# A query's own scores and weights: from five 512-column fp32r products to 32-column fp32 products and a round trip through device memory

## The chip, the cores and the metric

The kernel runs on one core of one Trainium2 chip. The metric is the device time of one execution in microseconds (us), lower is better; the times given are the median of three executions and, for the trace, the one execution that was profiled.

## What is computed

The reference applies two conditional residual layers to `x` (8 batches of 512 rows by 512 features). The change lies in the first, an attention layer with 16 heads of 32 features:

```python
query = seq2 + b_self
key   = concatenate([seq1 + b_prev, seq2 + b_self], 1)      # seq1 = x, seq2 = the side input
value = concatenate([seq1, seq2], 1)
q, k, v = query @ Wq + bq, key @ Wk + bk, value @ Wv + bv   # split in 16 heads of 32
score_prev = einsum('bhqd,bhkd->bhqk', q, k[:, :, :512]) * SCALE      # masked behind seq_len1
score_self = (q * k[:, :, 512:]).sum(-1, keepdims=True) * SCALE       # one score per query: its own key
weights = softmax(concatenate([score_prev, score_self], -1))
attn = einsum(weights[..., :-1], v[:, :, :512]) + weights[..., -1:] * v[:, :, 512:]
x = x + (attn @ Wo + bo)
```

So each query has 512 scores against the previous sequence and one score against itself (the **own score**). The second layer is an MLP with a shared and an expert part, `gelu(x @ W1 + b1) @ [W2 | We[index]]`, added to `x`. The change does not touch it.

## The kernel before

**Stages.** Everything stands transposed: features on the 128 partitions, the 512 rows of a batch along the free axis. The first stage computes the attention of all 8 batches and writes it to device memory; the second does the output projection, the residual and the MLP. Products that need precision are made of three fp32r products (high by high, high by low, low by high parts).

**Runs.** The attention stage is a sequence of 32 *runs*, one for each batch b and group g of four heads (g is 0 to 3; C = 4 groups in a batch, G = 4b + g counts them). The functions `batch` of each engine (TensorE from line 1220, ScalarE 664, VectorE 925, GpSimd 528, SyncE's queue 374) are loops over g with 16 *steps* i inside. The first and the last batch are unrolled, the six between them are a hardware loop. Nothing is scheduled at run time: each engine works down its own list, and semaphores hold it where its input isn't there. In what follows "run g" is the run of group g in a middle batch and "step i" one of its 16 steps.

**What TensorE does in a step.** One score tile of the present group (`score_tile`, line 1167: keys 128t to 128t+127 of head j against 512 queries, i = 4t + j); at most two `max_tile` products of the *next* group (1129; VectorE's `maximum`, 826, takes the row maxima off them, and product n waits until maximum n-2 is made), 16 in steps 0 to 9; from step 4 a third of one of four projections for the group after the next (`project`, 1084, four products a step); at steps 1, 5, 9 and 13 a `value_burst` (1176: four fp32 products of probabilities by values, each in 32 columns of the array), at step 5 also `denominators` (1189: four of the same form). In run 0 of a batch steps 1 to 4 hold also `values` (1114: 12 products each). The score tile of step i waits until ScalarE has made the probabilities of step i-2, since there are two banks of scores.

**The softmax bound and the own score.** The exponent is taken relative to a bound per query, the larger of its maximum over the keys and its own score. For the next group this is prepared in the present run:
- VectorE's `qk` (813) makes q times own key, `qk_f`; ScalarE's `qk_high` (578, step 1 of the next run) and VectorE's `qk_low` (822, step 5) split it into fp32r parts.
- At step 10 TensorE's `own_scores` (1142) sums it over each head's 32 features: two products of 512 columns with the 4-column matrix `sum_heads`, into 4 rows of `ps_max[1]`. `turn_max` (1150) turns the column maxima `m_col` into 4 rows of `ps_max[0]` by four fp32 products of 128 columns with the identity.
- ScalarE's `own_row` (589) copies the 4 rows, VectorE's `max_row` (835) takes the larger, ScalarE's `m_high` (595) and VectorE's `m_low` (842) make the negative high and low part in `m_neg`, and ScalarE's queue issues two DMAs (`maxima`, 603, at step 12) that put them into two rows of `q_st`, from where the score products subtract them. The first score tile of the next run waits for them (`m_landed`, 1171).
- At step 13 TensorE's `own_less_max` (1157) makes own score minus bound on all 128 rows at once: two products with the 128x128 block matrix `sum_spread` and one of `spread` by `m_neg`. ScalarE's `own_weight` (611, step 15) takes the exponential of it into `den`, waiting first for VectorE's `normalize` (884) of step 14, which frees that half of `den`.
- In the next run GpSimd's `own_value` (493, step 3) multiplies the own values by it, VectorE's `numerator` (847, step 3) and `denominator` (856, step 7) add it in. The first burst of that run waits for `numerator`, which frees `ps_num`.

**SyncE's queue** holds in each run the DMAs that stack the parts of the group after the next (`stack`, 311: three of 128 KB for each of four heads, and one row of the mask for groups 0 and 1), which wait for `q_low` at step 11; in run 1 also the loads of the next batch (`load`, 301), of which two are placed before head 0's and two before head 2's stacks; and last `store` (325) of the group before. ScalarE has in runs 1 and 2 also the `in_high` casts of the next batch, VectorE their transposes and GpSimd their low parts.

Of the kernel before, what the change touches and what calls it, by code (L numbers as in the profile page):

```python
# [19 lines left out]
def cond_resid_program(nc, x, seq2, prev_len, expert, Wq, bq, Wk, bk, Wv, bv, Wo, bo, b_prev, b_self,  # L20
# [16 lines left out]
    KE = DH + HG  # L37
# [3 lines left out]
    attn_dram = nc.dram_tensor("attn_scratch", (B, C, P, S), F32, kind="Internal").ap()  # L41
    mask_dram = nc.dram_tensor("mask_scratch", (B, S), F32, kind="Internal").ap()
# [15 lines left out]
    with keep:  # L58
# [37 lines left out]
        spread_f = before.enter_context(nc.sbuf_tensor("spread_f", [KE, P], F32))  # L96
# [16 lines left out]
        qk_hi = sb1("qk_hi", [P, S], F32R)  # L113
        qk_lo = sb1("qk_lo", [P, S], F32R)
        m_row = sb1("m_row", [HG, S])
        m_neg = sb1("m_neg", [KE, S], F32R)
        m_col = sb1("m_col", [P, C, HG])
        sum_heads = sb1("sum_heads", [P, HG], F32R)
        sum_spread = sb1("sum_spread", [P, P], F32R)
        spread = sb1("spread", [KE, P], F32R)  # L120
# [65 lines left out]
        qk_f_made, qk_hi_made, qk_lo_made = sem("qk_f_made"), sem("qk_hi_made"), sem("qk_lo_made")  # L186
# [5 lines left out]
        m_row_made, m_hi_made, m_lo_made = sem("m_row_made"), sem("m_hi_made"), sem("m_lo_made")  # L192
        m_landed = [sem(f"m_landed{r}") for r in range(2)]
        ow_mm, ow_made = sem("ow_mm"), sem("ow_made")
# [99 lines left out]
        def _(sp):  # L294
# [29 lines left out]

            def store(b, c):
# [42 lines left out]
            for j in range(HG):  # L368
                stack(0, 1, j)
            for dst, src in ((bv_col[:, :], bv), (bo_col[:, :], bo), (bias_1[:, :], b1), (bias_2[:, 0:CS], b2)):  # L370
# [104 lines left out]
        def _(pool):  # L475
            pool.memset(ident_f[:, :], 0.0).then_inc(consts_made, 1)
            pool.memset(spread_f[:, :], 0.0).then_inc(consts_made, 1)
            pool.iota(pos_i[:, :], pattern=[[1, S]], base=0, channel_multiplier=0).then_inc(consts_made, 1)
            pool.wait_ge(consts_made, 2)
            pool.affine_select(out=ident_f[:, :], in_=ident_f[:, :], compare_op=ALU.not_equal, fill=1.0, base=0,  # L480
                               pattern=[[-1, P]], channel_multiplier=1).then_inc(consts_made, 1)
            for n in range(2):

                pool.wait_ge(consts_made, 4 + n)
                pool.affine_select(out=spread_f[:, :].rearrange("k (j d) -> k j d", d=DH),
                                   in_=spread_f[:, :].rearrange("k (j d) -> k j d", d=DH),
                                   compare_op=ALU.not_equal, fill=1.0, base=-QUAD * n,
# [859 lines left out]
```

## Time and profile before

| | |
|---|---|
| median of 3 executions | 1920.85 us (1918.96 to 1922.35) |
| the profiled execution | 1924.15 us, span in the trace 1922.3 us |
| TensorE busy (PE) | 1838.3 us, 96% of the span |
| VectorE (DVE) busy | 965.4 us, 50% |
| ScalarE (ACT) busy | 752.9 us, 39% |
| GpSimd (POOL) busy | 636.2 us, 33% |
| mean granted TensorE clock | 0.977 of full |

The attention stage lasts from the start to about 1100 us, the MLP stage from there to the end. A run of groups 1 or 3 takes 28.8 us, a run of group 0 some 38.6 us, since it holds `values`. "PEld" are weight loads, which overlap the products; "ACTq" and "SPq" are the engines' queues, which issue DMAs in order with their other instructions. The printed duration of a product is longer than its place in the stream: two fp32r products of 512 columns that follow each other are printed with 0.39 us each and start 0.23 us apart, so the starts are to be read.

### The profile page before, as it was taken

How to read it: one execution, taken by the hardware profiler on the slowest of the kernel's cores; microseconds unless marked ns; L12 is line 12 of the kernel's file. 1: busy time of each engine (PE TensorE's matmuls, PEld its weight loads, DVE VectorE, ACT ScalarE, POOL GpSimd, SP SyncE). 2: the span in 40 equal slices, each digit the busy share in tenths (PEclk: the TensorE clock that was granted, in tenths of full speed). 3: DMA queues.
4: the chain of work that ended last, by engine and by line, in shares of the span. 5: the costliest groups of instructions: out<-in, count | busy, mean ns of one | idle time of the engine just before them, and what ended most of it. 6: DMA issues, size and time to landing. Idle time of an engine off the chain costs nothing.

```text
span 1922.3 us, 27293 instructions
## 1 busy us (share of the span) xinstructions
PE 1838.3 (96%) x8288; PEld 1300.6 (68%) x8288; DVE 965.4 (50%) x1373; ACT 752.9 (39%) x1290; POOL 636.2 (33%) x492
## 2 busy tenths in 40 slices
PE   6999999999999999999998799999999999999997
PEld 5656656556566565565564378888888888888886
DVE  4576576775775757757757552313232323232311
ACT  3354454444544544445434432323333332323222
POOL 3276484674764846747646400000000000000000
PEclk8999999999999999999999599999999999999999
DMA  6152342431623324316223431212131212122111
GB/s 142 35 116 57 70 83 71 78 82 39 121 59 73 78 67 82 77 40 120 64 53 88 126 94 39 50 38 50 33 55 33 50 37 38 47 33 51 27 22 22
DMA packets 337244, 122.17 MB, mean 64 GB/s; under 512 B 285642, under 2 KB 304074, under 8 KB 337170
## 3 DMA queue, kind: packets, MB, share of 16 engines
q1 hardware_dynamic: 336658, 120.83, 29.3%
q10 hardware_dynamic: 512, 0.53, 0.1%
q8 instruction: 26, 0.43, 0.1%
q14 instruction: 48, 0.39, 0.1%
HBM read 53.63 MB, written 16.79 MB: 37 GB/s over the span
## 4 chain that ended last, share of the span: by engine, by line
PE 85%; DVE 5%; issue 3%; POOL 3%; ACT 2%; SPq 2%; DMA 1%; ACTq 1%; DVEq 0%; POOLq 0%
PE ps_proj L1109 17%; PE ps_av L1061 6%; PE ps_av L1063 6%; PE ps_av L1062 6%; PE ps_av L1186 6%; PE ps_max L1139 6%; PE ps_score L1173 5%; PE ps_proj L1061 3%; PE ps_max L1063 3%; PE ps_score L1063 3%; PE ps_score L1062 3%; PE ps_max L1062 3%; PE ps_max L1061 3%; PE ps_score L1061 3%; PE ps_proj L1062 3%
## 5 line engine op out<-in xcount | busy, mean ns | idle before, releaser
L626 ACT ACTIVATE p_f<-ps_score 128x512 f32<-128x512 f32 x512 | 305.7, 599 | 499.3 <-PE ps_score L1173 415.7
L832 DVE TENSOR_REDUCE m_col<-ps_max 128x1 f32<-128x512 f32 x512 | 331.6, 684 | 237.8 <-PE ps_max L1139 237.4
L510 POOL TENSOR_TENSOR p_sum<-p_sum,p_f 128x512 f32<-128x512 f32 x256 | 344.1, 1357 | 113.8 <-ACT p_f L626 112.8
L994 DVE TENSOR_TENSOR h_lo<-h_f,h_hi 128x512 fp32r<-128x512 f32 x128 | 88.3, 690 | 480.0 <-ACT h_hi L723 479.9
L507 POOL TENSOR_TENSOR p_sum<-p_f 128x512 f32<-128x512 f32 x128 | 163.1, 1296 | 267.7 <-PE ps_av L1195 260.0
L1173 PE MATMUL ps_score<-stacks 99*128 99x512 f32 x512 | 216.8, 426 | 10.3 <-ACT p_f L626 9.6
L1139 PE MATMUL ps_max<-stacks 97*128 97x512 f32 x512 | 190.7, 428 | 31.6 <-DVE m_col L832 28.5
L1109 PE MATMUL ps_proj<-in_hi,w_hi 128*128 128x512 f32 x512 | 208.0, 406 | 10.9 <-POOL in_lo L515 7.6
L1109 PE MATMUL ps_proj<-in_lo,w_hi 128*128 128x512 f32 x512 | 206.4, 403 | 0.0
L1109 PE MATMUL ps_proj<-in_hi,w_lo 128*128 128x512 f32 x512 | 206.2, 403 | 0.0
L1061 PE MATMUL ps_av<-y_hi,w_hi 128*128 128x512 f32 x512 | 199.4, 390 | 1.5 <-DVE y_lo L990 1.5
L1063 PE MATMUL ps_av<-y_hi,w_lo 128*128 128x512 f32 x512 | 199.2, 389 | 0.0
L1062 PE MATMUL ps_av<-y_lo,w_hi 128*128 128x512 f32 x512 | 199.2, 389 | 0.0
L721 ACT ACTIVATE h_f<-ps_av,bias 128x512 f32<-128x512 f32 x128 | 88.2, 689 | 243.1 <-PE ps_av L1063 216.5
L723 ACT ACTIVATE h_hi<-ps_av,bias 128x512 fp32r<-128x512 f32 x128 | 88.2, 689 | 208.2 <-PE ps_max L1063 208.2
L1139 PEld LDWEIGHTS ps_max<-stacks 97*128 97x128 f32 x512 | 97.5, 190 | 104.6 <-DVE m_col L832 85.6
L1186 PE MATMUL ps_av<-p_f,v_st 128*32 128x512 f32 x1024 | 144.3, 627 | 5.0 <-ACT p_f L626 4.9
L1173 PEld LDWEIGHTS ps_score<-stacks 99*128 99x128 f32 x512 | 97.5, 191 | 74.9 <-ACT p_f L626 39.7
L1109 PEld LDWEIGHTS ps_proj<-in_hi,w_hi 128*128 128x128 f32 x512 | 97.9, 191 | 55.1 <-issue 32.8
L1109 PEld LDWEIGHTS ps_proj<-in_hi,w_lo 128*128 128x128 f32 x512 | 97.6, 191 | 45.4 <-issue 25.2
L1109 PEld LDWEIGHTS ps_proj<-in_lo,w_hi 128*128 128x128 f32 x512 | 97.9, 191 | 41.5 <-issue 25.1
L882 DVE RECIPROCAL den<-den 128x128 f32<-128x128 f32 x128 | 112.2, 918 | 0.7
(129 smaller groups left out, 2863.3 us busy)
## 6 DMA issues: line engine op xcount, KB each, us to landing
stacks<-parts SPq DMA_DIRECT2D x384, 128.0 KB
raw<-in_x_dram SPq DMA_DIRECT2D x128, 64.0 KB, 2.1
raw<-in_fside_BxSxS_dram SPq DMA_DIRECT2D x128, 64.0 KB, 2.2
attn_scratch<-num SPq DMA_DIRECT2D x32, 256.0 KB, 2.3
x_raw<-in_x_dram SPq DMA_DIRECT2D x128, 64.0 KB, 2.1
a_raw<-attn_scratch SPq DMA_DIRECT2D x32, 256.0 KB, 3.2
we_raw<-in_L_cond_We_dram SPq DMA_DIRECT2D x32, 256.0 KB, 2.8
out_dram<-z_t SPq DMA_DIRECT2D x128, 64.0 KB, 1.9
```

The costliest lines, as they stand in the source:

```text
L507: pool.tensor_tensor(p_sum[:, j], p_f[:, j], now, ALU.add).then_inc(sum_made, 1)
L510: pool.tensor_tensor(p_sum[:, j], p_sum[:, j], now, ALU.add).then_inc(sum_made, 1)
L626: act.activation(p_f[:, i % FLIGHT], ps_score[i % 2][:, :], ACT.Exp, scale=SCALE).then_inc(p_made, 1)
L832: dve.tensor_reduce(m_col[:, n % C, n // C:n // C + 1], ps_max[n % 2][:, :], AX.X, ALU.max).then_inc(max_made, 1)
L882: dve.reciprocal(den[:, r, at], den[:, r, at]).then_inc(rden_made, 1)
L1061: pe.matmul(ps, left[0], right[0], start=first, stop=False)
L1062: pe.matmul(ps, left[0], right[1], start=False, stop=False)
L1063: return pe.matmul(ps, left[1], right[0], start=False, stop=last)
L1109: mm = pe.matmul(ps, left, right, start=(m == 0), stop=(m == 3 * C - 1))
L1139: pe.matmul(ps_max[n % 2][:, :], q_st[0:KM, r, j, P * t:P * (t + 1)], k_st[0:KM, r, j, :], start=True, stop=True).then_inc(max_mm, 1)
L1173: pe.matmul(ps_score[i % 2][:, :], k_st[0:KS, r, j, P * t:P * (t + 1)], q_st[0:KS, r, j, :], start=True, stop=True).then_inc(score_mm, 1)
L1186: pe.matmul(ps_num[at, :], v_st[:, t, P * g + DH * j:P * g + DH * (j + 1)], p_f[:, i % FLIGHT], start=(t == 0), stop=(t == C - 1)).then_in ...
```

## The change

It replaces the 4-row tiles of own scores and maxima by one 128x128 tile: row 32t + j, column q is head j, query 128t + q.
- `own_scores` becomes four fp32 products of 128 columns, one for each quarter t, each into 32 rows of `ps_max[1]`; `turn_max` likewise into `ps_max[0]`. `sum_heads` and `m_col` are 32 columns wide, zero beyond the fourth. `qk_hi`, `qk_lo`, `qk_high` and `qk_low` go.
- `own_less_max` goes from TensorE; VectorE subtracts on the 128x128 tile. ScalarE takes the exponential in place and stores the tile to device memory, and SyncE's queue spreads each head's row to 32 rows of `den` with four DMAs.
- `maxima` issues eight DMAs (quarter t, high or low) where it issued two.
- TensorE's value bursts and the denominators stand one step later and behind the projections, VectorE's `numerator` and `denominator` one step later. At step 10 the burst stands right before `own_scores` and `turn_max`.

```diff
+    own_dram = nc.dram_tensor("own_scratch", (2, C, DH, P), F32, kind="Internal").ap()
...
+            def own_weights(b, c):
+                G, r = C * b + c, c % 2
+                sp.wait_ge(ow_stored, DMA * (G + 1))
+                wait(sp, attn_made, G - 1)
+                for j in range(HG):
+                    sp.dma_start(den[DH * j:DH * (j + 1), r].rearrange("d (t q) -> d t q", q=P),
+                                 own_dram[r, :, j].partition_broadcast(DH)).then_inc(ow_landed[r], DMA)
...
@@ SyncE, batch: behind the stacks, before store
+                    if not (last and g == C - 1):
+                        own_weights(*after(b, g, 1))
...
@@ GpSimd
             def own_value(b, c):
-                pool.wait_ge(ow_made, G + 1)
+                pool.wait_ge(ow_landed[c % 2], HG * DMA * (2 * b + c // 2 + 1))
...
@@ ScalarE
-            def qk_high(b, c):
...
-                act.copy(m_row[:, :], ps_max[1][0:HG, :]).then_inc(own_made, 1)
+                wait(act, ow_stored, DMA * G)
+                act.copy(own_s[:, :], ps_max[1][:, 0:P]).then_inc(own_made, 1)
...
-                act.mul(m_neg[0:HG, :], m_row[:, :], -1.0).then_inc(m_hi_made, 1)
+                act.mul(m_neg[:, 0], m_s[:, :], -1.0).then_inc(m_hi_made, 1)
...
                 for n in range(2):
-                    act.dma_start(f(q_st[KM + n:KM + n + 1, r]),
-                                  f(m_neg[QUAD * n:QUAD * n + HG])).then_inc(m_landed[r], DMA)
+                    for t in range(C):
+                        act.dma_start(f(q_st[KM + n:KM + n + 1, r, :, P * t:P * (t + 1)]),
+                                      f(m_neg[DH * t:DH * t + HG, n])).then_inc(m_landed[r], DMA)
 
             def own_weight(b, c):
-                act.wait_ge(ow_mm, G + 1)
-                wait(act, attn_made, G - 1)
-                act.activation(den[:, c % 2], ps_max[1][:, :], ACT.Exp, scale=SCALE).then_inc(ow_made, 1)
+                act.wait_ge(own_less_made, G + 1)
+                act.activation(own_s[:, :], own_s[:, :], ACT.Exp, scale=SCALE).then_inc(ow_made, 1)
+                pb, pc = after(b, c, -2)
+                wait(act, ow_landed[c % 2], HG * DMA * (2 * pb + pc // 2 + 1))
+                act.wait_ge(ow_made, G + 1)
+                act.dma_start(own_dram[c % 2].rearrange("t k q -> (t k) q"), own_s[:, :]).then_inc(ow_stored, DMA)
...
@@ VectorE
-            def qk_low(b, c):
...
-                dve.tensor_tensor(m_row[:, :], ps_max[0][0:HG, :], m_row[:, :], ALU.max).then_inc(m_row_made, 1)
+                dve.tensor_tensor(m_s[:, :], ps_max[0][:, 0:P], own_s[:, :], ALU.max).then_inc(m_s_made, 1)
...
+            def own_less_max(b, c):
+                dve.wait_ge(m_s_made, C * b + c + 1)
+                dve.tensor_tensor(own_s[:, :], own_s[:, :], m_s[:, :], ALU.subtract).then_inc(own_less_made, 1)
...
-                        if i == 3 and started:
+                        if i == 4 and started:
                             numerator(*after(b, g, -1))
-                        if i == 7 and started:
+                        if i == 8 and started:
                             denominator(*after(b, g, -1))
...
@@ TensorE
-                pe.matmul(ps_max[1][0:HG, :], sum_heads[:, :], qk_hi[:, :], start=True, stop=False)
-                pe.matmul(ps_max[1][0:HG, :], sum_heads[:, :], qk_lo[:, :], start=False, stop=True).then_inc(own_mm, 1)
+                for t in range(C):
+                    mm = pe.matmul(ps_max[1][DH * t:DH * (t + 1), 0:P], sum_heads[:, :], qk_f[:, P * t:P * (t + 1)],
+                                   start=True, stop=True)
+                mm.then_inc(own_mm, 1)
...
-                    mm = pe.matmul(ps_max[0][0:HG, P * t:P * (t + 1)], m_col[:, t, :], f(ident[:, :]), start=True, stop=True)
+                    mm = pe.matmul(ps_max[0][DH * t:DH * (t + 1), 0:P], m_col[:, t, :], f(ident[:, :]), start=True, stop=True)
...
-            def own_less_max(b, c):
...
-                        if i == 1 and not (first and g == 0):
-                            value_burst(*after(b, g, -1), C - 1)
-                        if i > 1 and i % HG == 1:
-                            value_burst(b, g, i // HG - 1)
-                        if i == HG + 1 and not (first and g == 0):
-                            denominators(*after(b, g, -1))
                         if g == 0 and not first and 1 <= i < 1 + C:
                             values(b, i - 1)
                         if more and i >= 4:
                             project(*nxt2, order[(i - 4) // 3], (i - 4) % 3)
+                        if i == 2 and not (first and g == 0):
+                            value_burst(*after(b, g, -1), C - 1)
+                        if i > 2 and i % HG == 2:
+                            value_burst(b, g, i // HG - 1)
+                        if i == HG + 2 and not (first and g == 0):
+                            denominators(*after(b, g, -1))
                         if bound and i == 10:
                             own_scores(*nxt)
                             turn_max(*nxt)
-                        if bound and i == 13:
-                            own_less_max(*nxt)
```

## Rows read from the trace of the kernel before

**Rows 1.** The page's busy times, and the window of a run 3.

```profile
PE 1838.3 (96%) x8288; PEld 1300.6 (68%) x8288; DVE 965.4 (50%) x1373; ACT 752.9 (39%) x1290; POOL 636.2 (33%) x492
...
419.60:448.40 28.80, 28.08 (x135) 16.56 (x134) 21.19 (x29) 13.60 (x25) 16.97 (x14) 1.00 0.28 65
```

**Rows 2.** TensorE's timeline, run 3, steps 10 to 14: start, duration, instruction.

```profile
438.69 0.40 PE L1147 MATMUL ps_max<-qk_hi,sum_heads 128*4 128x512 f32 x1
...
439.25 1.04 PE L1154 MATMUL ps_max<-ident,m_col 128*4 128x128 f32 x8
440.22 0.50 PE L1173 MATMUL ps_score<-stacks 99*128 99x512 f32 x1
440.56 0.40 PE L1109 MATMUL ps_proj<-in_lo,w_hi 128*128 128x512 f32 x1
...
444.99 0.39 PE L1163 MATMUL ps_max<-qk_hi,sum_spread 128*128 128x512 f32 x1
...
445.98 0.50 PE L1173 MATMUL ps_score<-stacks 99*128 99x512 f32 x1
```

**Rows 3.** TensorE's timeline, run 3, step 5: a burst, the denominators, then projections.

```profile
427.43 1.06 PE L1186 MATMUL ps_av<-p_f,v_st 128*32 128x512 f32 x8
428.31 1.04 PE L1195 MATMUL ps_av<-p_sum,ones 128*32 128x512 f32 x8
429.29 0.50 PE L1109 MATMUL ps_proj<-in_lo,w_hi 128*128 128x512 f32 x1
429.62 0.39 PE L1109 MATMUL ps_proj<-in_hi,w_lo 128*128 128x512 f32 x1
```

**Rows 4.** TensorE's timeline, run 2: the score tiles of steps 12 and 15.

```profile
412.65 0.40 PE L1173 MATMUL ps_score<-stacks 99*128 99x512 f32 x1
...
418.42 0.39 PE L1173 MATMUL ps_score<-stacks 99*128 99x512 f32 x1
```

**Rows 5.** ScalarE's timeline, run 2: probabilities 12, the two DMAs, probabilities 13.

```profile
413.08 0.60 ACT L626 ACTIVATE p_f<-ps_score 128x512 f32<-128x512 f32 x1
414.63 1.22 ACTq L608 DMA_DIRECT2D stacks<-m_neg  x2
416.05 0.60 ACT L626 ACTIVATE p_f<-ps_score 128x512 f32<-128x512 f32 x1 [2.37 <-POOL p_sum L510]
```

**Rows 6.** DMA issues by line: duration on the queue in ns, minimum, median, maximum.

```profile
L608 ACTq DMA_DIRECT2D stacks<-m_neg x64: 580/587/1182, 69.4 to 1052.2; - x64
...
L323 SPq DMA_DIRECT2D stacks<-parts x384: 552/598/2155, 37.8 to 1028.0; - x192
...
L308 SPq DMA_DIRECT2D raw<-in_x_dram x128: 316/348/1792, 2.7 to 881.4; - x128
```

**Rows 7.** SyncE's queue, run 2: the last three of the stacks' DMAs.

```profile
420.97 1.87 SPq L323 DMA_DIRECT2D stacks<-parts  x3
```

**Rows 8.** The page's DMA issues: KB each, median us to landing.

```profile
raw<-in_x_dram SPq DMA_DIRECT2D x128, 64.0 KB, 2.1
...
attn_scratch<-num SPq DMA_DIRECT2D x32, 256.0 KB, 2.3
```

**Rows 9.** GpSimd's and VectorE's timelines, start of run 3, and all maxima by line.

```profile
421.21 1.28 POOL L498 TENSOR_TENSOR v<-v,den 128x512 f32<-128x512 f32 x1
...
425.67 0.68 DVE L853 TENSOR_TENSOR num<-ps_av,v 128x512 f32<-128x512 f32 x1
...
L832 DVE TENSOR_REDUCE m_col<-ps_max 128x1 f32<-128x512 f32 x512 | 331.6, 684 | 237.8 <-PE ps_max L1139 237.4
```

**Rows 10.** A product's idle time at the start of run 2, and windows.

```profile
389.91 0.49 PE L1139 MATMUL ps_max<-stacks 97*128 97x512 f32 x1 [0.79 <-DVE m_col L832]
...
396.00:398.00 2.00, 2.00 (x9) 0.90 (x8) 1.75 (x4) 0.83 (x2) 1.21 (x1) 0.50 0.07 26
398.00:400.00 2.00, 2.00 (x17) 0.49 (x16) 1.37 (x3) 0.27 (x1) 0.00 (x0) 0.68 0.00 0
...
779.50:781.00 1.50, 1.50 (x5) 1.11 (x5) 1.08 (x2) 0.00 (x0) 1.07 (x1) 0.50 0.01 3
```

More of the change, by code:

```diff
@@ L36, in cond_resid_program @@
     KS = KM + 2
-    KE = DH + HG
     QUAD = 32
@@ L191, in cond_resid_program @@
         turn_mm = sem("turn_mm")
-        m_row_made, m_hi_made, m_lo_made = sem("m_row_made"), sem("m_hi_made"), sem("m_lo_made")
+        m_s_made, m_hi_made, m_lo_made = sem("m_s_made"), sem("m_hi_made"), sem("m_lo_made")
         m_landed = [sem(f"m_landed{r}") for r in range(2)]
-        ow_mm, ow_made = sem("ow_mm"), sem("ow_made")
+        own_less_made, ow_made = sem("own_less_made"), sem("ow_made")
+        ow_stored = sem("ow_stored")
+        ow_landed = [sem(f"ow_landed{r}") for r in range(2)]
         score_mm = sem("score_mm")
@@ L476, in _ @@
             pool.memset(ident_f[:, :], 0.0).then_inc(consts_made, 1)
[L477 removed]
             pool.iota(pos_i[:, :], pattern=[[1, S]], base=0, channel_multiplier=0).then_inc(consts_made, 1)
[L479 removed]
+            pool.wait_ge(consts_made, 1)
             pool.affine_select(out=ident_f[:, :], in_=ident_f[:, :], compare_op=ALU.not_equal, fill=1.0, base=0,
                                pattern=[[-1, P]], channel_multiplier=1).then_inc(consts_made, 1)
[L482 to L487, printed above, removed]
[L488 removed]
+            pool.wait_ge(consts_made, 3)
             pool.memset(f(stacks[KM - 1:KS, 1]), 1.0).then_inc(ones_made[1], 1)
@@ L576, in v2_out @@
                 act.copy(v2[:, c], ps_proj[0][:, :]).then_inc(v2_made, 1)
-            def qk_high(b, c):
-                G = C * b + c
-                act.wait_ge(qk_f_made, G + 1)
-                wait(act, ow_mm, G)
-                act.copy(qk_hi[:, :], qk_f[:, :]).then_inc(qk_hi_made, 1)
             def v_out(b, t):
@@ L649, in _ @@
             weights_high(2)
-            qk_high(0, 0)
             v2_out(0, 0)
@@ L676, in batch @@
                             v2_out(*nxt)
-                        if i == 1 and maximum:
-                            qk_high(*nxt)
                         if g == 0 and not first and 2 <= i < 2 + C:
@@ L912, in _ @@
             weights_low(2, 2)
-            qk_low(0, 0)
             for t in range(3 * C):
@@ L921, in _ @@
             qk(0, 1)
-            max_row(0, 0)
+            own_max(0, 0)
             m_low(0, 0)
+            own_less_max(0, 0)
             def batch(b, first, last):
@@ L934, in batch @@
                                 maximum(*nxt, n)
-                        if i == 5 and bound:
-                            qk_low(*nxt)
-                        if i == 3 and started:
+                        if i == 4 and started:
                             numerator(*after(b, g, -1))
-                        if i == 7 and started:
+                        if i == 8 and started:
                             denominator(*after(b, g, -1))
@@ L951, in batch @@
                             m_low(*nxt)
+                            own_less_max(*nxt)
                         if i in (10, 13) and started:
@@ L1170, in score_tile @@
                 if i == 0:
-                    pe.wait_ge(m_landed[r], 2 * DMA * (2 * b + g // 2 + 1))
+                    pe.wait_ge(m_landed[r], 2 * C * DMA * (2 * b + g // 2 + 1))
                 wait(pe, p_made, T - 1)
@@ L1214, in _ @@
             values(0, 1)
-            own_less_max(0, 0)
             values(0, 2)
```

64 lines of the change are left out of this document (23 added, 41 removed).

## The prediction

> **What bounds the kernel now.** First the page's busy times and one run's window: TensorE is busy in 96% of the span, and in a run 3 of 28.8 us in 28.1, while VectorE, ScalarE and GpSimd stand at 75% of that window or less [rows 1]. So TensorE's stream sets the time, and what leaves it is gained, as long as nobody else is then late. Second, that stream itself, read by its starts. A product of 512 columns takes 0.23 us. I count a run 3 by this: 16 score tiles, 16 maxima and 48 projections are 80 x 0.23 = 18.5 us; four bursts of 1.2 us, 4.8; the denominators 0.9; what the change touches 2.7 (below). That is 26.9 of 28.8; the other 1.9 us are short stalls, nearly all in steps 0 to 5, where TensorE has few projections and waits for VectorE's maxima at 0.65 us each. Third, ScalarE in steps 12 to 15, the only place where the change puts more work on an engine's queue than it takes away.
>
> **Removed from TensorE.** From the first own product to the score tile behind the turned maxima are 440.22 - 438.69 = 1.53 us, and the product behind that tile starts 0.34 us after it and not 0.23: 1.64 us [rows 2]. `own_less_max`: 445.98 - 444.99 = 0.99, and 0.11 again: 1.10 us [rows 2]. Together 2.74 us a run.
>
> **Added there.** Eight fp32 products of 128 columns, each four in four different 32-column blocks. No row shows these. The denominators have this form with 512 columns: the burst's four take 0.88 us before them, in which the four ran side by side, since the turned maxima, four products of 128 columns in one and the same block, take 0.97 us for a quarter of the columns [rows 2, 3]. A quarter of 0.88 is 0.22 us for each set of four: 0.44. The upper bound is that they don't run side by side: 2 x 0.97 = 1.94. I take 0.44, as rows 3 have the same form. They stand behind a burst and cost no change of form of their own. The bursts are only moved: five places of 1.2 us or less, as before. **Net on TensorE: 2.74 - 0.44 = 2.3 us a run, 32 runs: -74 us.**
>
> **ScalarE's queue.** This is where I expect the gain to go. `maxima` issues eight DMAs for two. The two take 1.22 us back to back, and the probabilities of step 13 come only behind them [rows 5]. What would eight smaller ones take? An issue of 8 KB takes 0.587 us there, one of 128 KB on SyncE's queue 0.598; the cheapest loads from device memory take 0.316 [rows 6]. So it is the price of an instruction and not of its bytes, and both 0.59 rows go from SBUF to SBUF, as the new ones do. I take 0.61 each: 4.9 us; the lower bound is 0.32 each, 2.5 us.
> The path: score tile 12, then 0.43 us to its probabilities (412.65 to 413.08), 0.6 us for them, 4.9 us of issues, 0.2 to the next activation (415.85 to 416.05), 0.6 for probabilities 13 and 0.05 for the signal: 6.8 us until score tile 15 may start [rows 4, 5]. (The low part is ready by then: on 128 columns VectorE's small steps cost less than on 512.) TensorE has three steps of 5 x 0.23 and one burst between them, 4.65 us; before, it needed 5.77 [rows 4], with `own_less_max` among it. So it stands idle for 2.15 us, in 31 runs: **+66 us**. In run 1 two `in_high` casts (0.6 us each) stand on the same stretch; half of that has no cover: +0.7 x 8 = +6.
>
> By the Trainium skill (DMA: Bandwidth & Descriptors, Rules for kernel authors) small transfers should be coalesced, since under 64 KB one pays mostly overhead. The trace agrees in the issue times above, 0.587 us for 8 KB. If an issue went by its bytes instead, the eight would cost what the two cost, 1.2 us, and the term of 66 us would be nothing.
>
> **Step 15.** Exponential and store (0.3 and 0.4 us, the latter like other issues to device memory) stand before probabilities 15, which score tile 1 of the next run needs. ScalarE's wait for `normalize` goes to SyncE's queue. From probabilities 13 on: 14, exponential, store, 15 are 2.1 us, against 1.15 + 0.7 us on TensorE: +0.35 x 31 = **+11**.
>
> **Steps 0 to 5.** The burst leaves step 1 for step 2 and then stands under maxima already queued; the `qk_low` and `qk_high` passes go. I reckon VectorE's chain as 4.8 us from tile 0 to tile 4 for 5.3 now, and some of it comes back at maximum 7: -0.7 in 16 runs (1 and 3; run 2 has transposes there): **-11**. In run 0 `v_out` needs the burst that now stands behind `values(1)`: `values(2)` waits burst end + copy (0.6) less three products (0.7) and signals, 0.5 x 7: **+4**.
>
> **The own weight's way through memory.** Counted from score tile 15: probabilities 13 end with it, the store is issued 1.3 us later, lands 2.3 us on [rows 8] (3.6). SyncE's queue: its last stack waits for score tile 15 and has three issues, 1.9 us [rows 7]; with the mask rows it is full till about 3.2. Then four loads at 0.35 to 0.54, landing 2.1 after the last issue [rows 6, 8]: 7.1. GpSimd's product 1.3, so `numerator` can start at 8.5 and ends at 9.2 [rows 9], which is 8 us behind score tile 0. Now GpSimd's product starts 1.7 us behind that tile (421.21; the tile is at 419.56) and the numerator at 6.1 [rows 9]. VectorE stands before maximum 8 so long, and TensorE's product 10 (step 6, 8.5 us behind tile 0) needs it: about +0.5 us in run 1, 0.7 in run 3. In run 2 SyncE has 8 loads more before the last stacks, but GpSimd is behind there already: +1.0. Run 0 hides it behind `values`. 2.2 x 8 = **+18**. Bounds: 0 and 2.5 us in each of 24 runs, +60.
> At step 6 the denominators are 1.6 us later; GpSimd's first sum of `p` then is ready about 0.5 us before probabilities 8 want it: 0.
>
> **The clock.** In run 2 TensorE waited 0.79 us and twice more [rows 10], and then the granted clock stood at 0.50 for 2 us and at 0.68 over the next 2: 0.5 x 2 + 0.32 x 2 = 1.6 us lost [rows 10]. 0.50 is the lower of its two levels, 1.2 for 2.4 GHz. I find three such falls in the middle of the stage, near 140, 396 and 780 us, the last in these rows too. The new kernel idles 2.15 us in one piece at step 14: some more falls, six or so: **+10**.
>
> **Sum:** -74 + 66 + 6 + 11 - 11 + 4 + 18 + 10 = +30. Against the profiled execution 1924 + 30 = 1954; the median lies 3.3 lower: **1951 us**, 1.6% slower. What a measurement can tell from no change is about 0.2%, 4 us.
>
> **Rivals.**
> - *Issues are cheap* or there is slack that I don't see: at 0.32 us each ScalarE needs 4.4 us for the 4.65, so the 66, the 6 and most of the 11 go: 1951 - 80 = 1871; at 0.47 some 1910. For it: loads at 0.316. Against: the same line now shows a minimum of 0.580 in 64 issues. It ends faster; it decides below 0.49 us an issue (0.12 x 8 = 1 us less a run), where the sum is zero. With smaller errors of the other terms in the same direction, 0.34, centre 1895.
> - *The clock follows the idle stretch* in most runs, not in a few: 25 falls of 1.6 us, +40, less my 10: 1981. For it: three falls, each behind idle time of this size. Against: in run 3, with idle pieces of 0.3 us, none. 0.15.
> - *The 32-column blocks queue up*: +1.5 x 32 = 48: 1999. Against: rows 3. 0.04.
> - *It cancels*: 0.08.
> - My forecast, 0.39, own range 1930 to 1970.
>
> Slower is 0.39 + 0.15 + 0.04 = 0.58, faster 0.34, same 0.08. Two in ten left out, one on each side, gives 1878 to 1990: the lower end takes in an issue price near 0.35 us [rows 6], the upper one the clock.
>
> **What would show it.** Line 608's successor: 256 issues at 0.58 us; score tile 15 idle about 2 us on ScalarE's probabilities in nearly every run; the page's four-block products x8 in about 0.22 us for a set; TensorE's share falling from 96% to about 93%; VectorE's numerator waiting for GpSimd, and that for the loads into `den`. Wrong if the issues take half, if TensorE doesn't wait at step 15, or if the stage ends before 1060 us.

## Result, and the profile after

The changed kernel takes 2066.7 us (median of four, 2061.4 to 2068.0) against 1921.0 for the kernel before on the same chip: ratio 1.0754 (95% interval 1.0733 to 1.0775), 146 us slower. I had forecast 30 us slower with an upper end of 1990: the sign is right, the size is far off. The profiled execution's span is 2064.7 us against 1922.3.

First the page of the changed kernel: the engines' busy time, and the chain that ended last.

```profile
PE 1835.2 (89%) x8384; PEld 1320.9 (64%) x8384; DVE 981.5 (48%) x1367; ACT 712.8 (35%) x1258; POOL 618.1 (30%) x489
...
PE 74%; ACTq 8%; DVE 6%; issue 5%; POOL 3%; ACT 2%; SPq 1%; DMA 1%; POOLq 0%; DVEq 0%
```

TensorE's busy time is 3 us less than before [rows 1], its share 89% for 96%. So its idle time rose by (2064.7 - 1835.2) - (1922.3 - 1838.3) = 145.5 us, which is all of the 142 us by which the span grew. But the busy time should have fallen by the 74 us of work removed. That it did not is seen in the groups of products that the change leaves alone (busy us, mean ns of one, idle time before):

```profile
L1157 PE MATMUL ps_score<-stacks 99*128 99x512 f32 x512 | 246.4, 482 | 164.7 <-ACT p_f L625 163.4 <-DMA stacks<-m_neg 1.2
L1101 PE MATMUL ps_proj<-in_hi,w_hi 128*128 128x512 f32 x512 | 215.3, 420 | 23.6 <-POOL in_lo L517 20.3
L1131 PE MATMUL ps_max<-stacks 97*128 97x512 f32 x512 | 208.8, 471 | 13.1 <-DVE m_col L821 12.7
```

The same three groups in the kernel before:

```profile
L1173 PE MATMUL ps_score<-stacks 99*128 99x512 f32 x512 | 216.8, 426 | 10.3 <-ACT p_f L626 9.6 <-DMA stacks<-m_neg 0.6
L1109 PE MATMUL ps_proj<-in_hi,w_hi 128*128 128x512 f32 x512 | 208.0, 406 | 10.9 <-POOL in_lo L515 7.6 <-DVE w_lo L796 3.2
L1139 PE MATMUL ps_max<-stacks 97*128 97x512 f32 x512 | 190.7, 428 | 31.6 <-DVE m_col L832 28.5
```

With the other two kinds of projection and the bursts, the unchanged products became 80 us dearer. Two things went wrong, then: a wait of 163 us before the score tiles, for ScalarE's probabilities (it was 10), and products that take longer, which is the clock. Where on TensorE, in runs 1 and 2:

```profile
435.92 0.80 PE L1157 MATMUL ps_score<-stacks 99*128 99x512 f32 x1 [8.91 <-ACT p_f L625]
...
462.16 0.40 PE L1140 MATMUL ps_max<-qk_f,sum_heads 128*32 128x128 f32 x8
462.38 0.40 PE L1148 MATMUL ps_max<-ident,m_col 128*32 128x128 f32 x8
...
471.58 0.57 PE L1157 MATMUL ps_score<-stacks 99*128 99x512 f32 x1 [2.96 <-ACT p_f L625]
```

The four-block products cost what I gave them: the sets start 0.22 us apart. Score tile 15 waits 2.96 us at the end of run 2, near my 2.15, but 8.91 in run 1. By run of a batch it is 3.7, 8.9, 2.9 and 3.6 to 4.9 us.

Now VectorE, GpSimd and ScalarE in that run 1 (start, duration, instruction). VectorE:

```profile
423.47 0.25 DVE L829 TENSOR_TENSOR m_s<-ps_max,own_s 128x128 f32<-128x128 f32 x1
423.65 5.89 DVE L799 TENSOR_TENSOR parts<-q_f,parts 128x512 fp32r<-128x512 f32 x1
429.46 0.28 DVE L833 SCALAR_TENSOR_TENSOR m_neg<-m_s,m_neg 128x128 fp32r<-128x128 f32 x1
```

GpSimd, whose instructions stand back to back from 420.28 to 429.00 us:

```profile
422.77 1.29 POOL L512 TENSOR_TENSOR p_sum<-p_sum,p_f 128x512 f32<-128x512 f32 x1
424.02 1.29 POOL L517 TENSOR_TENSOR in_lo<-turned,in_hi 128x512 fp32r<-128x512 f32 x1
...
427.74 1.26 POOL L512 TENSOR_TENSOR p_sum<-p_sum,p_f 128x512 f32<-128x512 f32 x1
436.45 1.28 POOL L517 TENSOR_TENSOR in_lo<-turned,in_hi 128x512 fp32r<-128x512 f32 x1 [7.46 <-ACT in_hi L555]
```

ScalarE:

```profile
423.76 0.31 ACT L596 ACTIVATE m_neg<-m_s 128x128 fp32r<-128x128 f32 x1 [0.94 <-DVE m_s L829]
...
429.77 5.30 ACTq L604 DMA_DIRECT2D stacks<-m_neg  x8
435.27 0.60 ACT L625 ACTIVATE p_f<-ps_score 128x512 f32<-128x512 f32 x1 [10.21 <-issue]
```

`q_low`, a subtraction of two SBUF tensors, is given 5.89 us and ends 0.5 us after GpSimd's last instruction. `m_low` (L833) stands behind it, the eight issues wait for `m_low`, and probabilities 13 for the issues. The same instruction over all runs, after, with `m_low` and the issues (ns, minimum, median, maximum):

```profile
L799 DVE TENSOR_TENSOR parts<-q_f,parts x32: 679/1758/5898, 37.3 to 1153.8; 128x512 fp32r<-128x512 f32 x32
...
L833 DVE SCALAR_TENSOR_TENSOR m_neg<-m_s,m_neg x32: 277/1372/1382, 68.1 to 1189.8; 128x128 fp32r<-128x128 f32 x32
...
L604 ACTq DMA_DIRECT2D stacks<-m_neg x256: 580/597/1177, 70.0 to 1195.2; - x128
```

and `q_low` before:

```profile
L806 DVE TENSOR_TENSOR parts<-q_f,parts x32: 668/669/691, 36.7 to 1019.1; 128x512 fp32r<-128x512 f32 x32
```

The Trainium skill (SBUF — State Buffer, Who interferes with whom) says that a VectorE instruction with two SBUF inputs and a GpSimd instruction that reads SBUF exclude each other, and that one with at most one SBUF input, outside its two-port modes, does not contend. The rows agree in kind: `m_s` (L829), which reads PSUM too, takes 0.25 us beside the same GpSimd stream, and `m_low`, of the same size but with both operands in SBUF, 1.37 in the median, about one GpSimd instruction more. The page lets the loser wait until the winner's instruction ends; here `q_low` waited over the rest of one and four more that followed it.

The kernel before shows the same hold, where it costs little. Its `m_low` (four rows of 512, both operands in SBUF) and its `normalize`:

```profile
L844 DVE SCALAR_TENSOR_TENSOR m_neg<-m_row,m_neg x32: 680/1455/1603, 67.8 to 1050.8; 4x512 fp32r<-4x512 f32 x32
...
L888 DVE TENSOR_TENSOR num<-num,den x32: 676/1754/1807, 130.7 to 1110.5; 128x512 f32<-128x512 f32 x32
```

In the run of rows 5 it is:

```profile
413.14 1.46 DVE L844 SCALAR_TENSOR_TENSOR m_neg<-m_row,m_neg 4x512 fp32r<-4x512 f32 x1 [0.30 <-ACT m_neg L601]
```

Probabilities 12 end at 413.68 there and the two DMAs start at 414.63, when `m_low` ends [rows 5]. So in the trace of before ScalarE already waited 0.95 us for the low part, and the same 512 columns took from 0.68 to 1.60 us.

Last the clock, around the same wait. The columns are the window, its length, then busy time and count of TensorE, its weight loads, VectorE, ScalarE and GpSimd, then the granted clock, the DMA share and GB/s.

```profile
424.00:425.50 1.50, 1.50 (x8) 1.14 (x7) 1.50 (x1) 1.07 (x3) 1.50 (x3) 1.00 0.00 0
434.50:436.00 1.50, 0.08 (x1) 0.08 (x1) 0.00 (x0) 0.73 (x2) 0.00 (x0) 0.50 0.82 147
...
446.50:448.00 1.50, 1.50 (x4) 1.22 (x5) 1.50 (x4) 1.10 (x2) 1.02 (x1) 0.51 0.12 44
448.00:449.50 1.50, 1.50 (x8) 1.19 (x8) 1.12 (x2) 0.63 (x2) 1.50 (x2) 1.00 0.00 0
```

After the idle stretch TensorE ran at half clock, the lower level, for twelve us, although it was busy. I cut the stage from 70 up to 1060 us into such windows and summed length x (1 - clock): 102 us in 33 falls, against 11 us in 5 falls before. The cut is not the same part of both kernels: the last score tile starts at 1081.5 us before and at 1229.8 in the changed kernel, so 170 us of slow stage are left out there. By the whole trace, span x (1 - mean granted clock), it is 2064.7 x (1 - 0.924) = 157 us against 1922.3 x (1 - 0.977) = 44. Some of this is idle time, which loses nothing, so it goes with the 80 us above.

### The profile page after: what moved, and what is told of

It is laid out like the page before. It is cut to its first block, busy times and chain, and to the rows that moved or that the text cites. A ratio compares the mean times of both kernels' runs of the same rounds, so it can differ in the third digit from the quotient of the medians.

```text
span 2064.7 us, 27779 instructions
## 1 busy us (share of the span) xinstructions
PE 1835.2 (89%) x8384; PEld 1320.9 (64%) x8384; DVE 981.5 (48%) x1367; ACT 712.8 (35%) x1258; POOL 618.1 (30%) x489
## 4 chain that ended last, share of the span: by engine, by line
PE 74%; ACTq 8%; DVE 6%; issue 5%; POOL 3%; ACT 2%; SPq 1%; DMA 1%; POOLq 0%; DVEq 0%
PE ps_proj L1101 12%; ACTq L604 8%; PE ps_max L1131 7%; PE ps_av L1053 6%; PE ps_score L1157 6%; PE ps_av L1055 6%; PE ps_av L1054 6%; PE ps_av L1170 5%; PE ps_score L1053 3%; PE ps_max L1053 3%; PE ps_max L1054 3%; PE ps_score L1054 3%; PE ps_max L1055 3%; PE ps_score L1055 3%; PE ps_proj L1053 3%
## 5 line engine op out<-in xcount | busy, mean ns | idle before, releaser
L1157 PE MATMUL ps_score<-stacks 99*128 99x512 f32 x512 | 246.4, 482 | 164.7 <-ACT p_f L625 163.4
L512 POOL TENSOR_TENSOR p_sum<-p_sum,p_f 128x512 f32<-128x512 f32 x256 | 332.0, 1323 | 139.4 <-ACT p_f L625 138.9
L1157 PEld LDWEIGHTS ps_score<-stacks 99*128 99x128 f32 x512 | 112.9, 221 | 288.9 <-ACT p_f L625 202.2
L1101 PE MATMUL ps_proj<-in_hi,w_hi 128*128 128x512 f32 x512 | 215.3, 420 | 23.6 <-POOL in_lo L517 20.3
L1131 PE MATMUL ps_max<-stacks 97*128 97x512 f32 x512 | 208.8, 471 | 13.1 <-DVE m_col L821 12.7
L1101 PE MATMUL ps_proj<-in_hi,w_lo 128*128 128x512 f32 x512 | 218.7, 427 | 0.0
L1101 PE MATMUL ps_proj<-in_lo,w_hi 128*128 128x512 f32 x512 | 214.7, 419 | 0.0
L1131 PEld LDWEIGHTS ps_max<-stacks 97*128 97x128 f32 x512 | 112.4, 220 | 84.8 <-DVE m_col L821 62.0
L1101 PEld LDWEIGHTS ps_proj<-in_hi,w_lo 128*128 128x128 f32 x512 | 106.7, 208 | 22.8
L1101 PEld LDWEIGHTS ps_proj<-in_lo,w_hi 128*128 128x128 f32 x512 | 104.0, 203 | 22.2
```

The costliest lines, as they stand in the source:

```text
L512: pool.tensor_tensor(p_sum[:, j], p_sum[:, j], now, ALU.add).then_inc(sum_made, 1)
L1101: mm = pe.matmul(ps, left, right, start=(m == 0), stop=(m == 3 * C - 1))
L1131: pe.matmul(ps_max[n % 2][:, :], q_st[0:KM, r, j, P * t:P * (t + 1)], k_st[0:KM, r, j, :], start=True, stop=True).then_inc(max_mm, 1)
L1157: pe.matmul(ps_score[i % 2][:, :], k_st[0:KS, r, j, P * t:P * (t + 1)], q_st[0:KS, r, j, :], start=True, stop=True).then_inc(score_mm, 1)
```

## Experiments

Medians of three rounds, each with its ratio to the kernel before on the same chip and the 95% interval. "Clock loss" is the sum just described, from 70 to 1060 us in each kernel, although their stages end at different times; where it bears on the argument the figure by the whole trace stands beside it.

**Eight issues in the kernel before.** Everything else as before, so no product is removed and nothing is moved.

```diff
-                    act.dma_start(f(q_st[KM + n:KM + n + 1, r]), f(m_neg[QUAD * n:QUAD * n + HG]))
+                    for t in range(C):
+                        act.dma_start(f(q_st[KM + n:KM + n + 1, r, :, P * t:P * (t + 1)]),
+                                      f(m_neg[QUAD * n:QUAD * n + HG, P * t:P * (t + 1)]))
```

> The kernel before with eight DMAs instead of two for the bounds on ScalarE's queue, nothing else. If the number of issues is the main cost of the change (0.61 us each, six more in each of 31 runs), score tile 15 waits some 2 us a run and the time rises by 60 us or more, with clock falls to about 2000 us. If the cost of the change is VectorE waiting for GpSimd or the own weight's way through memory, this is near 1921 us, at most 1950.

2029.5 us, 1.0566 (1.0548 to 1.0583). Its ScalarE queue and its score tile 15:

```profile
446.36 5.00 ACTq L609 DMA_DIRECT2D stacks<-m_neg  x8
...
452.20 0.79 PE L1174 MATMUL ps_score<-stacks 99*128 99x512 f32 x1 [1.89 <-ACT p_f L627]
```

The six added issues cost 108 us by themselves: 1.7 to 2.7 us of idle time before tile 15 in nearly every run, and clock loss 61 us in 18 falls (by the whole trace 101 us for 44). In the profiled execution (span 2026.5 us, TensorE busy 1891.1) idle time is 51 us up and busy time 53, with the same products. The term that I had as the largest is real; its companion, the clock, is as large.

**The order put back.** The changed kernel with the bursts, denominators, numerator and denominator at the steps of before.

```diff
-                        if i > 2 and i % HG == 2:
+                        if i > 1 and i % HG == 1:
                             value_burst(b, g, i // HG - 1)
-                        if i == HG + 2 and not (first and g == 0):
+                        if i == HG + 1 and not (first and g == 0):
                             denominators(*after(b, g, -1))
```

> The changed kernel with bursts, denominators, numerator and denominator back in their old steps. If the later denominators give GpSimd its backlog, which starves VectorE's q_low in run 1 (5.9 us a piece), then q_low falls back under 2 us there, the idle time before score tile 15 in run 1 falls from 9 to about 4 us, and the time to about 2020 us. If the order of the bursts has no part in it, the time stays within 10 us of 2067, or rises since own scores lose their place behind a burst (0.2 us x 31 = 6 us).

2013.1 us, 1.0480 (1.0463 to 1.0498): 54 us come back. Its `q_low` and `m_low`:

```profile
L799 DVE TENSOR_TENSOR parts<-q_f,parts x32: 679/682/961, 36.8 to 1098.5; 128x512 fp32r<-128x512 f32 x32
...
L833 DVE SCALAR_TENSOR_TENSOR m_neg<-m_s,m_neg x32: 292/1379/1390, 67.6 to 1132.6; 128x128 fp32r<-128x128 f32 x32
```

So `q_low`'s long form came from the new order, in which GpSimd's sums meet it back to back; `m_low`'s 1.4 us did not. Tile 15 now waits 4.3 us in run 1 and 2.5 to 2.8 in the others.

**Only the order changed, in the kernel before** (the same edit the other way round).

> The kernel before with only the bursts, the denominators, numerator and denominator in their new steps. I had put this at -11 us. If the later denominators cost by giving GpSimd a backlog, which then holds VectorE's q_low, the time rises by 10 to 40 us and q_low or m_low takes 4 us or more in run 1; if the moves only cost in the changed kernel, where own scores come earlier, it lies between 1905 and 1925 us.

1938.3 us, 1.0091 (1.0071 to 1.0111). I had -11 for the moves; they cost 17. `q_low` was 5.4 us once (0.67 to 0.69 in all runs of before) and `m_low` no longer than before, so the sign that I had named came once and not in every run 1; TensorE waited 19.8 us for `in_low` against 7.6, and eight times, 9.8 us in all, for the bounds' low part (once, 2.5 us, before).

**VectorE's small steps read PSUM.** The changed kernel, but `q_low` is formed from the projection in PSUM, and `m_s` lies in an unused part of a PSUM bank.

```diff
-                dve.tensor_tensor(q_lo[:, :], q_f[:, :], f(q_hi[:, :]), ALU.subtract)
+                dve.scalar_tensor_tensor(out=q_lo[:, :], in0=ps_proj[0][:, :], scalar=bias[:, 0, c:c + 1],
+                                         in1=f(q_hi[:, :]), op0=ALU.add, op1=ALU.subtract)
-        m_s = sb1("m_s", [P, P])
+        m_s = ps_max[0][:, P:2 * P]
```

> The changed kernel with VectorE's q_low reading the projection from PSUM and the maxima tile m_s kept in PSUM, so that none of the small steps between own scores and the DMA issues reads two operands from SBUF. If VectorE waits there for GpSimd's use of SBUF, q_low takes 0.75 us everywhere, m_low and the subtraction 0.3 us; idle before score tile 15 falls from 9 to about 4 us in run 1, by 1 us in the others: 2067 - 8 x 5 - 24 x 1 = about 2000 us. If those long durations have another cause, nothing changes (2067 within 5 us).

1960.3 us, 1.0195 (1.0178 to 1.0212): 106 us less than the changed kernel, where I had expected 67. VectorE, ScalarE's queue and score tile 15 at the end of run 2:

```profile
457.16 0.74 DVE L799 SCALAR_TENSOR_TENSOR parts<-ps_proj,bias,parts 128x512 fp32r<-128x512 f32 x1
458.07 0.29 DVE L834 SCALAR_TENSOR_TENSOR m_neg<-ps_max,m_neg 128x128 fp32r<-128x128 f32 x1 [0.17 <-ACT m_neg L596]
...
458.40 5.00 ACTq L604 DMA_DIRECT2D stacks<-m_neg  x8
...
464.24 0.50 PE L1159 MATMUL ps_score<-stacks 99*128 99x512 f32 x1 [1.68 <-ACT p_f L625]
```

This is the path I had predicted: 5.0 us of issues and 1.68 us idle (I had 4.9 and 2.15). The idle time before the score tiles is 83 us for 163, the clock loss 49 (by the whole trace 100 for 157). The wait of VectorE for GpSimd is the step that I had left out.

**The same with the order put back** (both edits).

> after_nolock with bursts, denominators, numerator and denominator in their old steps. If the order cost only through q_low and m_low being held by GpSimd, nothing is left of the 54 us that undoing it gave: 1960 within 10 us. If the order has a cost of its own (before_moves: 17 us, in run 1 to 2 alone), it falls by 15 us or more to about 1943 us.

1962.4 us, 1.0200 (1.0165 to 1.0234). With `q_low` out of GpSimd's way the order costs nothing in sum, within some 7 us: its 54 us were `q_low`'s wait and what that drew after it. Against the kernel with only the order put back (2013.1 us), where `q_low` was not held, the same edit gives some 50 us: those are `m_low`'s and not `q_low`'s, since in nearly every run its hold stood ahead of the issues (tile 15 waits 4.3 us in run 1 there and 3.2 here), with the clock behind it.

**`q_low` and the maxima from PSUM in the kernel before.**

> The kernel before with q_low reading PSUM and m_row kept in PSUM, the same edit as after_nolock made. Its q_low was never held (0.67 us in all runs), and m_low's 1.4 us has no one waiting behind it: 1921 us within 5. If it falls by 15 us or more, the gain of after_nolock over the changed kernel was not the removal of the change's own cost but a gain that the kernel before could have as well.

1920.3 us, 0.9983 (0.9973 to 0.9992): the edit is worth 3 us where `q_low` is never held. What it gives in the changed kernel is not a gain of its own.

**The bounds through device memory.** One store by ScalarE and four loads by SyncE in place of the eight issues.

```diff
-                for n in range(2):
-                    for t in range(C):
-                        act.dma_start(f(q_st[KM + n:KM + n + 1, r, :, P * t:P * (t + 1)]), ...)
+                act.dma_start(m_dram[r].rearrange("t k n q -> (t k) n q"), f(m_neg[:, :, :]))
+                for j in range(HG):
+                    sp.dma_start(f(q_st[KM:KM + 2, r, j].rearrange("n (t q) -> n t q", q=P)),
+                                 m_dram[r, :, j].rearrange("t n q -> n t q"))
```

> The changed kernel with the bounds going through device memory: one store issued by ScalarE, four loads by SyncE's queue between the stacks, in place of eight issues on ScalarE's queue. If the eight issues (5.2 us) are the main cost, score tile 15 waits less than 1 us in runs 0, 2 and 3, only run 1 keeps some 4 us from q_low, the clock stays up in most runs, and the time falls by 100 us or more, to between 1900 and 1960 us. If the issues only filled time in which ScalarE would have waited anyway, it stays above 2030 us.

2065.0 us, 1.0729 (1.0701 to 1.0757): a miss; nothing was gained. The wait for ScalarE fell from 163 to 31 us, but score tile 0 of the next run now waits 110 us for the loads. At the end of run 1, TensorE and SyncE's queue:

```profile
437.45 0.80 PE L1171 MATMUL ps_score<-stacks 99*128 99x512 f32 x1 [6.97 <-DMA stacks<-m_scratch]
```

```profile
430.74 4.28 SPq L308 DMA_DIRECT2D raw<-in_fside_BxSxS_dram  x8
435.14 1.18 SPq L330 DMA_DIRECT2D stacks<-m_scratch  x4
```

ScalarE issued the store at 427.87; SyncE came to the loads at 435.14, behind six stacks and eight loads of inputs. The issues of run 1 went from the engine that had no time to the one whose queue is in order. Behind runs 0 and 2 tile 0 waited about 1.9 and 1.8 us, behind run 3 2.5 to 5.0.

**Fillers for the clock.** In step 14 the changed kernel gets 12 more products of 512 columns (36 in run 1), written to a bank that nobody reads. They add work and take away no wait.

```diff
+                        if bound and more and i == 14:
+                            filler(*nxt, 36 if g == 1 else 12)
```

> The changed kernel with fillers: behind the burst of step 14 TensorE works through 12 needless products (36 in run 1) into ps_max[1], which is free there, where it would stand idle. If low clock costs time of its own beside the waits, the fillers keep the clock up and the time falls although TensorE has more to do: the granted clock goes from 0.92 to 0.96 or more and the time to 2020 us or less. If the low clock falls only into waiting time and costs nothing, the time stays at 2067 or rises a little.

2023.0 us, 1.0530 (1.0512 to 1.0547): 44 us faster with 552 more products. One such stretch:

```profile
448.40 3.02 PE L1157 MATMUL ps_max<-w_hi 128*128 128x512 f32 x12
```

The clock loss falls from 102 to 12 us (by the whole trace from 157 to 54). The waits of ScalarE's queue stand under the fillers, not gone; so what came back is the clock's part. It is a lower bound, since fillers longer than the wait cost time themselves: 44 us of the 146, net of the fillers, are clock; by the unchanged products' busy time it is some 80.

**The own weight's way left out.** The kernel with VectorE's steps from PSUM, without the store, the loads and the waits for them: the own position's weight in the output is left out (what `den` held before stands in its place).

> after_nolock without the own weight's way: neither stored nor loaded nor waited for, so that the output has wrong own weights (den holds old values in their place). If that way holds numerator and with it TensorE at step 6 (my +18 us, here GpSimd waits for it in every run), the time falls from 1960 by 15 to 50 us; if it is hidden, by less than 8 us (the 0.65 us of exponential's successor, the store's issue, in front of probabilities 15 are included).

1959.8 us, 1.0188 (1.0167 to 1.0209), against 1960.3: nothing. GpSimd waits 161 us for these loads in the changed kernel's trace, but nothing on TensorE's path waits for that in this kernel: my +18 was wrong. (Whether it would count once the issues' wait is gone too, no run shows.)

**Four issues.** The kernel with VectorE's steps from PSUM, without the low part of the bounds (the stack's last row stays at what it was; that part of the computation is left out), so four issues for eight.

> after_nolock with four issues instead of eight for the bounds: the low part of the bounds is left out (its row of q_st stays at 1.0), so that the output is slightly off. If the number of issues is what is left of the loss, ScalarE ends its issues 2.5 us sooner, the 1.7 us of idle before score tile 15 goes in every run and the low clock with it: 1960 - 31 x 1.7 - about 25 for the clock = 1880 us, within 15. If something else holds tile 15 or the 74 us of TensorE's work aren't there to be won, it stays above 1930 us.

1936.4 us, 1.0065 (1.0048 to 1.0081): a miss of 56 us. The wait before score tile 15 is gone, but in TensorE's waits a new one leads (us in total, times, longest), and VectorE's and TensorE's timelines show it once a batch:

```profile
PE ps_max L1133 <- DVE m_col L822: 58.3, 66, 6.1
```

```profile
390.89 6.91 DVE L882 TENSOR_TENSOR num<-num,den 128x512 f32<-128x512 f32 x1
...
399.06 0.79 PE L1133 MATMUL ps_max<-stacks 97*128 97x512 f32 x1 [5.93 <-DVE m_col L822]
```

Again a product of two SBUF tensors, held beside back-to-back GpSimd instructions, the rest of one and five more, up to 397.25. With eight issues the same line took 0.7 to 0.8 us at this place: it started at 396.31 us and GpSimd, which waited for ScalarE's casts behind the issues, had nothing from 396.52 to 399.05. The eight issues, by holding ScalarE's casts and so GpSimd, had kept this wait from arising.

**Four issues, and the denominator in PSUM.** Only that product is taken out of GpSimd's way.

```diff
-                dve.tensor_tensor(den[:, g % 2], ps_den[:, :], den[:, g % 2], ALU.add)
+                dve.tensor_tensor(ps_den[:, :], ps_den[:, :], den[:, g % 2], ALU.add)
-                dve.reciprocal(den[:, r, at], den[:, r, at])
+                dve.reciprocal(ps_den[:, at], ps_den[:, at])
-                dve.tensor_tensor(num[:, r], num[:, r], den[:, r], ALU.mult)
+                dve.tensor_tensor(num[:, r], num[:, r], ps_den[:, :], ALU.mult)
```

> This is the kernel with four issues of the bounds (which leaves out the bounds' low part, stack row KM+1), and besides the denominator's sum and its reciprocal stand in PSUM (ps_den), so that the product num x den reads one operand from PSUM and not both from SBUF; nothing else is changed. With four issues the run took 1936.4 us, where I had written 1880 +- 15. Its trace has no idle time left ahead of score tile 15, but once a batch (8 times) the product num<-num,den took 6.9 us in place of 0.7, beside back-to-back GpSimd instructions, and TensorE stood 5.9 us before the products for the maxima. Theory (the four issues gave back their time, and VectorE's wait for GpSimd came up in another instruction): 8 x 5.9 = 47 us go, 1889, within 1875 to 1900; num<-num,den at most 0.8 in runs 0 to 3 of every batch; TensorE's idle time before L1133 falls from 58 us to about 12. Rival (own weight's way through memory, or the clock, is what was left): 1925 to 1936, the idle time before L1133 or before the numerator stays. A smaller part by the clock: the five or six us of standing still each drop the clock for a while, so 5 to 10 us more could go.

1889.3 us, 0.9833 (0.9816 to 0.9849): 47 us less. The time is what the theory gave (8 x 5.9), but its make-up is not quite: the idle time before these products falls to 23.2 us and not to 12, TensorE's idle time by 35 us in all (from 1936.1 - 1799.3 to 1885.3 - 1783.6) and its busy time by 16, which I had put at 5 to 10. Its rows:

```profile
PE ps_max L1133 <- DVE m_col L822: 23.2, 76, 0.9
```

```profile
L882 DVE TENSOR_TENSOR num<-num,ps_av x32: 647/674/687, 127.9 to 1073.8; 128x512 f32<-128x512 f32 x32
```

TensorE's busy time of 1783.6 us is 55 less than before although the clock is lower (by the whole trace 66 us lost for 44), so the removed work is there as a gain. But this is not the whole change: the low part of the bounds is left out. And the denominator in PSUM wasn't tried in the kernel before, where the same product takes 1.75 us in the median; TensorE's waits for the maxima sum to 28.5 us there, none over 0.9. How much the kernel before would gain by that edit isn't shown.

**The parts that pay, in the layout of before.** The kernel before, with its two issues and four-row maxima, takes from the change the own weight's way through memory: `own_less_max` leaves TensorE for a subtraction by VectorE on four rows; `q_low` and the maxima come from PSUM; `numerator` stands one step later.

```diff
-                pe.matmul(ps, sum_spread[:, :], qk_hi[:, :], start=True, stop=False)
-                pe.matmul(ps, sum_spread[:, :], qk_lo[:, :], start=False, stop=False)
-                pe.matmul(ps, spread[:, :], m_neg[:, :], start=False, stop=True).then_inc(ow_mm, 1)
+                dve.tensor_tensor(own_s[:, :], own_s[:, :], m_row[:, :], ALU.subtract).then_inc(own_less_made, 1)
...
+                act.dma_start(own_dram[c % 2], own_s[:, :]).then_inc(ow_stored, DMA)
```

> The kernel before in its 4-row layout with two bounds DMAs, but without own_less_max on TensorE: the own weight is made on 4 rows by VectorE and ScalarE, stored and spread by four loads, m_row stands in PSUM and q_low reads PSUM. TensorE loses 1.10 us a run (-35 us). If eight issues and the two-operand reads are what costs, and the round trip costs little, it ends at 1890 to 1910 us, faster than both kernels. If the round trip is the cost, it ends above 1921.

1909.0 us, 0.9942 (0.9922 to 0.9962), the whole computation: 14 us (0.6%) below the kernel before. TensorE's busy time falls by the 35 us that I had written (1838.3 to 1803.3), but 15 us of idle time come in (1922.3 - 1838.3 to 1902.1 - 1803.3), spread over several waits; what draws them is open.

## Why the prediction was wrong, step by step

The direction was right and so was its main reason; the range was missed by 77 us because two terms that I had at 0 (VectorE's small steps) and at 10 (the clock) are of the size of the largest.

- **TensorE's work, -74: right.** The four-block sets take 0.22 us each. Busy time fell by 3 us while the unchanged products rose by 80, which makes 83 removed, by modelled ends. The rival of blocks that queue up fell.
- **ScalarE's queue, +66: right in mechanism and price.** 256 issues at 0.597 us (I had 0.61), eight in 5.0 us in the kernels where nothing holds them, 1.68 us idle for 2.15. 2 KB cost what 8 KB did, so the price goes by the number of issues and cheap issues, my rival of 0.34, fell.
- **"The low part is ready by then: on 128 columns VectorE's small steps cost less than on 512": this step failed.** I gave the small steps a duration by size and looked at no one beside them, though in the rows I used 0.95 us lie between probabilities 12 and the DMAs, which is the held `m_low`; my path left them out. They read two tensors in SBUF, and GpSimd was at work: `q_low` up to 5.9 us, `m_low` 1.37, both ahead of the issues. Read from PSUM, they give back 106 us, the clock that follows included: some 50 of it in the kernel where only `m_low` is held, the rest by `q_low`.
- **"At step 6 the denominators are 1.6 us later; ... 0", and the moves at -11: failed.** GpSimd's backlog in the run's last steps now meets `q_low`. The order costs 54 us in the changed kernel, 17 alone, and nothing in sum (1960.3 against 1962.4) once `q_low` reads PSUM. So the two failed steps are one mechanism, and the 54 are within the 106.
- **The clock, +10: far too small.** Loss 102 us in 33 falls for 11 in 5, by the whole trace 157 for 44. I priced a fall at 1.6 us from rows 10 and let six runs have one; it is 3 us in the mean, part of it in idle time, and up to 1060 us there are 33 falls for 27 waits at tile 15. My rival "the clock follows the idle stretch in most runs" came true, but I had it on idle stretches of 2 us and at 1.6 us a fall, so its 1981 was too low too.
- **The own weight's way, +18: nothing.** The loads are late, as I said, but no one on the path waits: leaving them out saves 0.5 us, within the intervals.
- **Step 15 (+11) and `v_out` (+4)** weren't measured by themselves. The first is also added up wrong: 2.1 us against 1.15 + 0.7 leave 0.25 us a run and not 0.35, +8 for 31 runs.

What the runs add up to: 2066.7, less 106 for the small steps, is 1960.3; less 71 for four of eight issues once the wait that came up without them is out too (24 and 47) is 1889.3, which is 32 below the kernel before, without the bounds' low part. Most of the gain of 74 was there (55 us less busy time at a lower clock); it was spent on ScalarE's queue, on VectorE's waits for GpSimd and on the clock that fell behind both. How far the 1889.3 could fall with the clock of before (66 for 44 us lost by the whole trace) is open, and so is what the order does to it.

Of what I said would show it: the issues and the x8 sets came as written, the waits at tile 15 came in nearly every run but at 2.7 us or more for my 2, TensorE's share fell to 89% and not to 93%, GpSimd did wait for the loads into `den`, but without effect.

## What to carry to other kernels

When instructions are moved on one engine, list the VectorE instructions with both operands in SBUF that run beside GpSimd: their recorded duration holds only for the neighbours that they had (0.67 to 6.9 us here), and one operand in PSUM freed them in both places where it was tried. A duration that differs between equal instructions in the trace of before is the sign to look for. Price an idle stretch on TensorE at its length plus the clock behind it, which here was half as much again (80 to 145 us) or as much again (eight issues in the kernel before). And when the first wait is taken away, expect a next one: four issues alone gave 24 of 71 us, since engines that the first wait had held apart now met.

## What the runs showed of the hardware that I had not expected

- A VectorE instruction with two SBUF operands was held over a whole chain of GpSimd instructions: 5.89 us over the rest of one and four more, 6.91 us over the rest of one and five more, where it takes 0.67 alone; in other runs the same instruction, or `m_low`, got in after one (1.76 and 1.37 us). What decides between the two isn't settled.
- An issue on ScalarE's queue from SBUF to SBUF costs 0.60 us for the 2 KB of the new ones, what it cost for 8 KB and what SyncE's 128 KB cost [rows 6]; the own weight's store to device memory takes 0.34.
- After 9 us of idle time TensorE stayed at the lower clock through twelve us of unbroken work (435.9 to 448.0); 552 useless products made the kernel 44 us faster.
